# Two chunks a Schur or solve step, side steps placed by readiness, and a turn's gelus in four pieces

## The chip, the cores and the metric

The kernel runs on one core of one Trainium2 chip. The metric is the device time of one execution in microseconds. The kernel before takes 1141.81 us (median of three runs, 1141.43 to 1143.41).

## What is computed

The input `x` is 4 x 1024 x 256. It is normalized, and goes through an attention block with a norm of its own and 16 heads of 64; the block's input and the input itself are added. A second block is a feed-forward net with binarized weights and 1024 hidden units. Cut to what matters:

```python
# per batch and head, over 8 chunks of 128 rows (Qc, Kc, Vc: 128 x 64)
G = Kc.T @ Kc + 1e-4 * I
W = solve(G, Kc.T @ Vc)
U = I[:, :8]
for _ in range(2):
    U, _ = qr(W @ U)
S = 0.9 * S + U @ (U.T @ W)          # carried from chunk to chunk
out = 0.125 * (Qc @ S)
# block: x + layernorm(x) + out @ Wo, then
# x + (gelu(layernorm(x) @ bin(w1).T + b1) @ bin(w2).T + b2),  bin(w) = mean|w| * sign(w)
```

All of it is float32; the feed-forward products use float16 halves (a high and a low part) of the data.

## The kernel before, in words

There are 32 chunks of 128 rows (8 for each of 4 batches). The work has three kinds, and one list, `ORDER`, holds every step. Each engine's program walks through that same list and emits its part of each step, so the list fixes the order on every queue. `plan()` (line 55) makes the list on the host, with estimated durations (`PE_WEIGHT`, `ACT_WEIGHT`, `DVE_WEIGHT`) for TensorE, ScalarE and VectorE, and also picks a pair of the eight PSUM banks for each step: `put` (line 110) takes the pair that is free first.

**Stage 1**, per chunk c: `T` (transposes of the normalized rows), `K` and `V` (projections, line 1107, eight 512-column matmuls each), `G` (32 small gram matmuls, line 1127). ScalarE copies each result out of PSUM (lines 732, 740, 751), SyncE's queue stores the gram to DRAM (line 547).

**Side chains.** The 64 x 64 grams are inverted by halves. For a batch, VectorE eliminates the 32 x 32 leading blocks of all 128 lane-chunks at once (a *sweep*: `SLOAD`, 32 pivots `PIV` at lines 960 to 977, `SSTORE`; GpSimd's queue loads and stores it). Then each chunk goes through the *Schur chain* on TensorE: `LC` (load, lines 501 and 506), `SP`, `SX`, `SV` (lines 1155, 1168, 1180). The Schur complements are swept in a second sweep. Then each chunk goes through the *solve chain*: `LS` (load of lps, vv, rr and cu, lines 519 to 526), `S`, `U`, `W`, `Y`, `YT`, `Z` (lines 1190, 1200, 1214, 1225, 1234, 1244). Between two steps of a chain stands a copy by ScalarE. When the eight chunks of a batch are through, `MLOAD`, `SML`, `MSTORE`, `MI` invert an 8 x 8 matrix for every lane-chunk on VectorE (the *small inverse*, lines 989 to 1012) and bring the result back. There are eight sweeps, (0, b) for the leading blocks of batch b and (1, b) for its complements, in the order (0,0) (0,1) (1,0) (0,2) (1,1) (0,3) (1,2) (1,3). They use two buffers in turn.

**Turns**, one per chunk r: `LF`, `NZ` (line 1257), `WRA` and `WRB` (line 1271, the operator's two halves; VectorE adds each to the decayed state at line 1027, or copies it at line 1024), `Q` (line 1117), `OT` (line 1284, attention), `WO` (line 1295), the norm on VectorE (lines 1038 to 1053, with a power on GpSimd, line 684), `Y3` (line 1306), `HID` (line 1318), `GE0` and `GE1` (four gelus and a cast each, lines 855 and 860), `LO0` and `LO1` (GpSimd, line 669), `OUT` (line 1328) and its end on VectorE (lines 1058 and 1062). Four turns overlap: the loop over r places NZ and Q of r+2, OT of r+1, WO of r, HID of r-1 and OUT of r-2.

**Where side steps go.** `host` places a step of stage 1 or of a turn, and after every 1.7 us of planned TensorE time a *slot*: up to three Schur steps of three successive chunks, or, if no Schur work is open, up to two solve steps of two successive chunks. Loads have two buffers (four for gct), so that one chunk's data come while another's are used. Before the turns of a batch, `wait_for_batch` places slots and nothing else until the batch's small inverse is planned to be done.

## Time and profile before

| | |
|---|---|
| median of the runs | 1141.81 us |
| the profiled execution | 1141.08 us |
| its span | 1139.3 us, 41225 instructions |
| TensorE busy | 976.5 us (86%) |
| TensorE weight loads | 732.9 us (64%) |
| VectorE busy | 650.0 us (57%) |
| ScalarE busy | 536.2 us (47%) |
| GpSimd busy | 196.8 us (17%) |
| mean granted clock of TensorE | 0.916 of full speed |
| the chain that ended last | PE 73%, DMA 7%, ACT 7%, issue 5%, SP's queue 4%, VectorE 4% |

The span is the time between the first and the last instruction. PE is TensorE, PEld its weight loads, DVE VectorE, ACT ScalarE, POOL GpSimd, SPq the queue of SyncE, which issues most DMAs. The granted clock is a share of full speed: 1.0 is 2.4 GHz, 0.5 is 1.2 GHz, a value between them a mean over a stretch with both.

### The profile page before, as it was taken

What the parts mean: (1) busy time and instruction counts of PE and PEld (TensorE: products, weight loads), DVE (VectorE), ACT (ScalarE), POOL (GpSimd) and SP (SyncE); (2) the same over time, 40 slices, a digit from 0 to 9 for tenths busy, and PEclk for the clock granted to TensorE, in tenths of its full rate; (3) what the DMA queues carried; (4) which work ended last, traced back from release to release, by engine and by line L of the source; (5) the groups of instructions that cost most, each with busy time, mean ns of one, the idle gap of its engine ahead of it and who ended that gap; (6) DMA issues with size and microseconds to landing.
All of it is one profiled execution on the core that took longest, in us unless ns stands there. A gap on an engine that the chain in (4) does not pass through costs nothing.

```text
span 1139.3 us, 41225 instructions
## 1 busy us (share of the span) xinstructions
PE 976.5 (86%) x18210; PEld 732.9 (64%) x18210; DVE 650.0 (57%) x1439; ACT 536.2 (47%) x1064; POOL 196.8 (17%) x246
## 2 busy tenths in 40 slices
PE   4898898996889986567988899899578989999997
PEld 2454445653545555446877788687456878888886
DVE  5772980999669995153675676588321243333333
ACT  2653334633544554342545544356444544444445
POOL 3431000010020001000122132221000232222223
PEclk9999999998999996677998999899656999999999
DMA  9543126634664576443144321423444121111100
GB/s 289 165 142 93 56 88 155 168 120 109 169 170 96 155 187 183 101 109 88 51 139 126 98 66 41 118 64 93 133 101 103 56 53 40 40 41 40 40 20 20
DMA packets 210912, 117.49 MB, mean 103 GB/s; under 512 B 145776, under 2 KB 197360, under 8 KB 209712
## 3 DMA queue, kind: packets, MB, share of 16 engines
q1 hardware_dynamic: 205264, 93.62, 31.3%
q0 software_dynamic: 5472, 21.24, 6.1%
q8 instruction: 145, 2.38, 0.9%
q14 instruction: 31, 0.25, 0.1%
HBM read 61.74 MB, written 53.08 MB: 101 GB/s over the span
## 4 chain that ended last, share of the span: by engine, by line
PE 73%; DMA 7%; ACT 7%; issue 5%; SPq 4%; DVE 4%; POOL 1%; POOLq 0%; DVEq 0%; ACTq 0%
PE psum L1107 19%; PE psum L1295 10%; PE psum L1117 9%; PE psum L1127 5%; PE psum L1328 5%; PE psum L1318 5%; PE psum L1214 3%; PE psum L1284 3%; DMA cu<-gc_d 3%; DMA schur_mem<-lead_d 2%; PE psum L1271 2%; PE psum L1200 2%; PE psum L1180 2%; ACT kv L740 2%; PE psum L1155 2%
## 5 line engine op out<-in xcount | busy, mean ns | idle before, releaser
L1107 PE MATMUL psum<-wqkv,xhat 128*128 128x512 f32 x512 | 241.0, 621 | 2.5 <-ACT xhat L732 2.3
L968 DVE SCALAR_TENSOR_TENSOR outer<-sweep_mem,rd 128x992 f32<-128x992 f32 (+30 forms) x248 | 187.4, 755 | 8.7
L974 DVE TENSOR_TENSOR sweep_mem<-sweep_mem,outer 128x992 f32<-128x992 f32 (+30 forms) x248 | 177.7, 716 | 8.5
L1107 PEld LDWEIGHTS psum<-wqkv,xhat 128*128 128x128 f32 x512 | 97.2, 197 | 115.5 <-issue 112.8
L740 ACT COPY kv<-psum 128x1024 f32<-128x1024 f32 x64 | 64.8, 1012 | 164.7 <-PE psum L1107 164.7
L1295 PE MATMUL psum<-wo,kv 128*128 128x256 f32 x512 | 124.4, 398 | 0.7 <-DVE state L1027 0.4
L1117 PE MATMUL psum<-xhat,wqkv 128*128 128x128 f32 x1024 | 124.6, 281 | 0.3 <-ACT nz L829 0.3
L669 POOL TENSOR_TENSOR hsplit<-gc,hsplit 128x512 f16<-128x512 f32 x64 | 74.6, 1166 | 284.9 <-ACT hsplit L860 284.8
L1117 PEld LDWEIGHTS psum<-xhat,wqkv 128*128 128x128 f32 x1024 | 120.6, 197 | 2.0 <-ACT nz L829 0.4
L1295 PEld LDWEIGHTS psum<-wo,kv 128*128 128x128 f32 x512 | 98.5, 197 | 16.1 <-DVE state L1027 0.6
L855 ACT ACTIVATE gc<-psum,b1c,alpha 128x128 f32<-128x128 f32 x256 | 96.8, 468 | 19.1 <-PE psum L1318 19.1
L746 ACT COPY ql<-psum 128x1024 f32<-128x1024 f32 x32 | 32.4, 1012 | 105.6 <-PE psum L1117 105.5
L1127 PE MATMUL psum<-kv 128*64 128x128 f32 x1024 | 63.3, 275 | 18.3 <-ACT kv L740 17.8
L1027 DVE SCALAR_TENSOR_TENSOR state<-state,psum 128x256 f32<-128x256 f32 x56 | 22.7, 419 | 89.6 <-PE psum L1271 87.1
L1127 PEld LDWEIGHTS psum<-kv 128*64 128x64 f32 x1024 | 56.0, 137 | 24.8 <-issue 24.7
L1038 DVE TENSOR_TENSOR gc<-psum,resl 128x256 f32<-128x256 f32 x32 | 13.6, 425 | 98.0 <-PE psum L1295 98.0
L1328 PE MATMUL psum<-s2t,hsplit 128*128 128x256 f16 x512 | 65.3, 282 | 4.5 <-POOL hsplit L669 2.7
L1318 PE MATMUL psum<-y3t,s1t 128*128 128x128 f16 x1024 | 63.3, 220 | 0.8 <-ACT y3t L844 0.8
L838 ACT ACTIVATE kv<-psum 128x1024 f32<-128x1024 f32 x32 | 32.8, 1024 | 64.0 <-PE psum L1284 63.6
L1318 PEld LDWEIGHTS psum<-y3t,s1t 128*128 128x128 f16 x1024 | 58.0, 98 | 6.4 <-issue 6.2
L1328 PEld LDWEIGHTS psum<-s2t,hsplit 128*128 128x128 f16 x512 | 48.9, 101 | 15.4 <-issue 4.1
L1214 PE MATMUL psum<-cu,rr 64*64 64x64 f32 x1024 | 43.1, 262 | 14.7 <-ACT cu L798 14.7
(117 smaller groups left out, 1389.0 us busy)
## 6 DMA issues: line engine op xcount, KB each, us to landing
gc_d<-gc SPq DMA_DIRECT2D x32, 512.0 KB, 3.4
schur_mem<-gc_d SPq DMA_DIRECT2D x32, 384.0 KB, 3.9
f_d<-fac SPq DMA_DIRECT2D x32, 272.0 KB, 2.2
fl<-f_d SPq DMA_DIRECT2D x32, 272.0 KB, 2.9
sv_d<-sv SPq DMA_DIRECT2D x32, 192.0 KB, 2.8
lead_d<-sweep_mem POOLq DMA_DIRECT2D x4, 1024.0 KB, 5.1
schur_mem<-lead_d SPq DMA_DIRECT2D x64, 64.0 KB, 3.7
r_d<-pt SPq DMA_DIRECT2D x32, 128.0 KB, 2.0
```

Source lines behind the costliest of these rows:

```text
L669: nc.gpsimd.tensor_tensor(hsplit[:, r % 2, 1, t].rearrange("p t r -> p (t r)"), ht[:, BANK * n:BANK * (n + 1)], hsplit[:, r % 2, 0, t].rea ...
L740: nc.scalar.copy(kv[:, n], place(step, c)).then_inc(drain(step, c), 1)
L855: nc.scalar.activation(ht[:, P * t:P * (t + 1)], place("HID", r)[:, P * t:P * (t + 1)], ACT.Gelu, scale=alpha1[:, t:t + 1], bias=b1c[:, t: ...
L968: V.scalar_tensor_tensor(out=tile, in0=a[:, t, t + 1:HALF].unsqueeze(2).broadcast_to([P, m, HALF]), scalar=rd[:, t:t + 1], in1=a[:, t, t + ...
L974: V.tensor_tensor(rest, rest, tile, ALU.subtract).then_inc(swept, 1)
L1107: ins = mm(dst[:, cols], xnt[:, c, t], wqkv[:, n, t, cols], start=t == 0, stop=t == KT - 1)
L1117: ins = mm(dst[:, cols], wqkv[:, 2, t, cols], xnt[:, TURNS[r], t], start=t == 0, stop=t == KT - 1)
L1127: ins = mm(dst[side(a), P * h:P * (h + 1)], kv[:, 0, cols], kv[:, :, cols], start=True, stop=True)
L1214: ins = mm(dst[side(a ^ n), at:at + HD], u if turned else r, r if turned else u, start=True, stop=True)
L1295: ins = mm(dst[:, 0:DM], ot[:, r % 2, at:at + P], wo[:, h], start=h == 0, stop=h == PAIRS - 1)
L1318: ins = mm(dst[:, P * t:P * (t + 1)], s1t[:, k, P * t:P * (t + 1)], y3t[:, part, k], start=k + part == 0, stop=k + part == KT)
L1328: ins = mm(dst[:, 0:DM], hsplit[:, r % 2, part, t], s2t[:, t], start=t + part == 0, stop=t + part == FT)
```

## The change

- `K`, `V` and `Q` become two steps of one bank each (`KA`, `KB`, ...), each with its own copy of 512 columns. The gram's first half waits for the first halves only.
- Every Schur step and every solve step but `W` covers two chunks (a pair e). Its matmuls and copies are those of both, its stores one DMA. `W` stays per chunk. The load buffers hold one pair at a time (gct two pairs), so that a load waits for the steps of the pair before: lps and vv for U, rr and cu for the second W.
- `host` no longer counts TensorE time: after every hosted step one Schur step and one solve step may follow, each only if its input is planned to be there (`ready`).
- The plan waits for inputs (`ready` in `put`), its weights are new, and pivots may be planned up to 1.2 us ahead of TensorE (`DVE_BEHIND`).
- `GE0` and `GE1` become `GE0` to `GE3`, two gelus each, the cast of a half behind every second. They stand between the copies of other steps. `WRA` and `WRB` of r+2 move from the start of the next pass to behind `QB` and behind `Y3`.

The core of the diff:

```diff
-BANKS = dict(T=1, K=2, V=2, Q=2, G=2, FT=2, FB=1, SP=1, SX=1, SV=1, S=1, U=2, W=2, Y=2, YT=1, Z=2,
+BANKS = dict(T=1, KA=1, KB=1, VA=1, VB=1, QA=1, QB=1, G=2, FT=2, FB=1, SP=1, SX=1, SV=2, S=1, U=2, W=2, Y=2, YT=1, Z=2,
              NZ=1, WRA=2, WRB=2, OT=2, WO=1, Y3=1, HID=2, OUT=1)
-PE_WEIGHT = dict(T=.25, K=3.45, V=3.45, Q=3.6, G=1.8, FT=.9, FB=.4, SP=.6, SX=.7, SV=.9, S=.5, U=.5, W=1.1, Y=.4, YT=.4,
-                 Z=.4, NZ=.4, WRA=.4, WRB=.4, OT=1., WO=3.5, Y3=.3, HID=1.9, OUT=1.9)
-ACT_WEIGHT = dict(T=.9, K=1.2, V=1.2, Q=1.2, G=1.2, FT=1.2, FB=.5, SP=.5, SX=1.8, SV=.6, S=.3, U=1.3, W=1.2, Y=.5, YT=.3,
-                  Z=.6, NZ=.4, OT=1.2, Y3=.7, GE0=2.5, GE1=2.5)
-DVE_WEIGHT = dict(WRA=.5, WRB=.5, WO=1.5, X3=1.3, OUT=.95)
-SIDE_EVERY = 1.7
+PE_WEIGHT = dict(T=.4, KA=1.75, KB=1.75, VA=1.75, VB=1.75, QA=1.8, QB=1.8, G=1.9, FT=.9, FB=.5, SP=.9, SX=1.1, SV=1.5, S=.6, U=.85, W=1.05,
+                 Y=.55, YT=.5, Z=.65, NZ=.55, WRA=.45, WRB=.45, OT=1.05, WO=3.65, Y3=.35, HID=1.9, OUT=1.8)
+ACT_WEIGHT = dict(T=.95, KA=.6, KB=.6, VA=.6, VB=.6, QA=.6, QB=.6, G=1.05, FT=1.05, FB=.4, SP=.6, SX=2.4, SV=.85, S=.4, U=2.1, W=1.05,
+                  Y=.8, YT=.35, Z=.7, NZ=.4, OT=1.05, Y3=.6, GE0=.95, GE1=1.6, GE2=.95, GE3=1.6)
...
+POOL_WEIGHT = dict(LO0=1.25, LO1=1.25)
+DVE_BEHIND = 1.2
...
-            j, at = staged[0]
-            start = max(now["dve"], at)
-            if start > now["pe"]:
+            j, loaded = staged[0]
+            start = max(now["dve"], loaded)
+            if start > now["pe"] + DVE_BEHIND:
                 return
...
+    def follows(step, c):
+        return dict(KA=[("T", c)], KB=[("T", c)], VA=[("T", c)], VB=[("T", c)], G=[("VB", c)], SP=[("LC", c)], SX=[("SP", c)],
+                    SV=[("SX", c)], S=[("LS", c)], U=[("S", c)], W=[("U", c // 2)] if step == "W" else [],
+                    Y=[("W", 2 * c + 1)] if step == "Y" else [], YT=[("Y", c)], Z=[("YT", c)], NZ=[("LF", c)],
+                    WRA=[("NZ", c)], WRB=[("NZ", c)], OT=[("WRB", c), ("QB", c)], WO=[("OT", c)], Y3=[("X3", c)],
+                    HID=[("Y3", c)], OUT=[("LO1", c)]).get(step, [])
+    def ready(step, c):
+        return max([0.0] + [at.get(e, 1e9) for e in follows(step, c)])
...
-            now["pe"] = max([now["pe"]] + free[k:k + n]) + PE_WEIGHT[step]
+            k = bank(n)
+            now["pe"] = max([now["pe"], min(ready(step, c), now["pe"] + 20.0)] + free[k:k + n]) + PE_WEIGHT[step]
             before[step, c] = [u for i, u in enumerate(held[k:k + n]) if u and u not in held[k:k + i]]
...
+    def load_schur():
+        e = chain["schur_next"]
+        if e < NCH // 2 and at.get(("swept", 0, e // half_batch), 1e9) <= now["pe"]:
+            put("LC", e)
+            chain["schur"] += [("SP", e), ("SX", e), ("SV", e)]
+            chain["schur_next"] += 1
...
+    def schur_step():
+        if not chain["schur"]:
+            load_schur()
+        if not chain["schur"] or ready(*chain["schur"][0]) > now["pe"]:
             return False
+        step, e = chain["schur"].pop(0)
+        put(step, e)
+        if step == "SP":
+            load_schur()
+        elif step == "SV" and e % half_batch == half_batch - 1:
+            open_at[1, e // half_batch] = at["SV", e] + 4.0
         return True
+    def load_solve():
+        e = chain["solve_next"]
+        if e < NCH // 2 and at.get(("swept", 1, e // half_batch), 1e9) <= now["pe"]:
+            put("LS", e)
+            chain["solve"] += [("S", e), ("U", e), ("W", 2 * e), ("W", 2 * e + 1), ("Y", e), ("YT", e), ("Z", e)]
+            chain["solve_next"] += 1
+    def solve_step():
+        if not chain["solve"]:
+            load_solve()
+        if not chain["solve"] or ready(*chain["solve"][0]) > now["pe"]:
             return False
+        step, e = chain["solve"].pop(0)
+        put(step, e)
+        if step == "W":
+            if e % 2 == 0:
+                put(*chain["solve"].pop(0))
+            load_solve()
+        elif step == "Z" and e % half_batch == half_batch - 1:
+            put("MLOAD", e // half_batch)
+            small_at[e // half_batch] = now["pe"] + 7.0
         return True
     def side():
+        done = [schur_step(), solve_step()]
+        return any(done)
...
     def host(step, c):
         put(step, c)
-        main[0] += PE_WEIGHT.get(step, 0.0)
-        if main[0] >= SIDE_EVERY:
-            main[0] = 0.0
-            side()
+        side()
...
-        if on(r + 1):
-            put("WRA", r + 1)
-            put("WRB", r + 1)
         if on(r - 2):
             put("LO1", r - 2)
         if on(r):
...
         if on(r + 2):
             load_factors(r + 2)
             host("NZ", r + 2)
+        if on(r - 1):
+            put("GE1", r - 1)
         if on(r - 2):
             host("OUT", r - 2)
         if on(r - 1):
+            put("GE2", r - 1)
             put("LO0", r - 1)
         if on(r + 2):
-            host("Q", r + 2)
+            host("QA", r + 2)
+        if on(r - 1):
+            put("GE3", r - 1)
+        if on(r + 2):
+            host("QB", r + 2)
+            put("WRA", r + 2)
         if on(r):
             host("Y3", r)
-        if on(r - 1):
-            put("GE1", r - 1)
+        if on(r + 2):
+            put("WRB", r + 2)
     return order, sweep_order, where, before
...
+            def load_solve(e):
+                b, c = e // HALF_BATCH, 2 * e
+                if e == 0:
                     sp.wait_ge(eyes_placed, 4)
+                if e % HALF_BATCH == 0:
                     sp.wait_ge(sweep_stored[J[1, b]], 16)
+                    sp.wait_ge(sv_stored, 16 * HALF_BATCH * (b + 1))
+                    sp.wait_ge(r_stored, 16 * HALF_BATCH * (b + 1))
+                if e:
+                    sp.wait_ge(*is_filled("U", e - 1))
+                for i in range(2):
+                    sp.dma_start(lps[:, i], comp_d[b].rearrange("(s c q) t n -> c (q t) s n", c=CPB, q=QUADS)[c % CPB + i]
+                                 ).then_inc(solve_loaded, 16)
+                    sp.dma_start(vv[:, i], sv_d[c + i][:, :, HALF:]).then_inc(solve_loaded, 16)
+                if e:
+                    sp.wait_ge(*is_filled("W", c - 1))
+                for i in range(2):
+                    sp.dma_start(rr[:, i, :, 0:HALF], r_d[c + i]).then_inc(solve_loaded, 16)
+                src = gc_d[c:c + 2].rearrange("c (s u) r n -> r u c s n", u=2)
                 for a in range(2):
+                    for u in range(2):
+                        sp.dma_start(cu[rows(2 * a), u], src[rows(2 * a), u, :, :, HD:P]).then_inc(solve_loaded, 16)
...
+            def lower_rows(e):
+                act.wait_ge(*is_filled("U", e))
+                if e:
+                    act.wait_ge(*is_filled("W", 2 * e - 1))
                 for a in range(2):
                     sl = rows(2 * a + 1)
+                    ins = nc.scalar.copy(cu[sl].rearrange("p u c s n -> p (u c s n)"), place("U", e)[sl])
+                ins.then_inc(drain("U", e), 1)
 
...
+                half = n // 2
                 if n == 0:
                     act.wait_ge(*is_filled("HID", r))
-                wait(act, low_done, 2 * (r - 1) + n + 1)
-                for t in range(4 * n, 4 * n + 4):
+                wait(act, low_done, 2 * (r - 1) + half + 1)
+                for t in range(2 * n, 2 * n + 2):
                     nc.scalar.activation(ht[:, P * t:P * (t + 1)], place("HID", r)[:, P * t:P * (t + 1)], ACT.Gelu,
                                          scale=alpha1[:, t:t + 1], bias=b1c[:, t:t + 1]).then_inc(gelu_done, 1)
+                if n % 2 == 0:
+                    return
                 if r >= 2:
                     act.wait_ge(*is_filled("OUT", r - 2))
-                act.wait_ge(gelu_done, FT * r + 4 * n + 4)
-                nc.scalar.copy(hsplit[:, r % 2, 0, 4 * n:4 * n + 4].rearrange("p t r -> p (t r)"),
-                               ht[:, BANK * n:BANK * (n + 1)]).then_inc(drain("HID", r) if n else high_done, 1)
+                act.wait_ge(gelu_done, FT * r + 4 * half + 4)
+                nc.scalar.copy(hsplit[:, r % 2, 0, 4 * half:4 * half + 4].rearrange("p t r -> p (t r)"),
+                               ht[:, BANK * half:BANK * (half + 1)]).then_inc(drain("HID", r) if half else high_done, 1)
...
-                for h in range(PAIRS):
-                    for a in range(2):
-                        cols = side(2 * h + a)
-                        ins = mm(dst[side(a), P * h:P * (h + 1)], kv[:, 0, cols], kv[:, :, cols], start=True, stop=True)
+                for half in range(2):
+                    pe.wait_ge(*is_drained(("KA", "KB")[half], c))
+                    pe.wait_ge(*is_drained(("VA", "VB")[half], c))
+                    for h in range(4 * half, 4 * half + 4):
+                        for a in range(2):
+                            cols = side(2 * h + a)
+                            ins = mm(dst[side(a), P * h:P * (h + 1)], kv[:, 0, cols], kv[:, :, cols], start=True, stop=True)
                 ins.then_inc(fill("G", c), 1)
```

## Rows read from the trace of the kernel before

**Rows 1.** Windows: stretch, length, each engine's busy us, then granted clock, DMA share, GB/s.
```profile
417.00:520.00 103.00, 58.57 (x2394) 46.62 (x2397) 43.25 (x96) 42.32 (x94) 9.69 (x15) 0.66 0.58 146
...
795.00:868.00 73.00, 48.10 (x1749) 36.96 (x1746) 18.06 (x60) 31.78 (x70) 4.99 (x9) 0.57 0.49 118
933.00:1113.00 180.00, 172.94 (x2476) 153.20 (x2464) 60.60 (x136) 89.05 (x181) 44.21 (x50) 1.00 0.13 37
```

**Rows 2.** Timeline of TensorE in stage 1: start us, length us, what, idle before.
```profile
101.89 7.13 PE L1107 MATMUL psum<-wqkv,xhat 128*128 128x512 f32 x16
...
110.22 1.97 PE L1127 MATMUL psum<-kv 128*64 128x128 f32 x32 [0.98 <-ACT kv L740]
112.12 7.13 PE L1107 MATMUL psum<-wqkv,xhat 128*128 128x512 f32 x16
```

**Rows 3.** Waits: who waited for whom, us in total, times, longest us.
```profile
PE psum L1190 <- DMA cu<-gc_d: 33.3, 9, 6.4
...
PE psum L1155 <- DMA schur_mem<-lead_d: 22.1, 8, 7.6
...
PE psum L1127 <- ACT kv L740: 17.8, 19, 1.0
```

**Rows 4.** Timeline of TensorE: the first NZ, and two turns at the end.
```profile
519.91 1.04 PE L1257 MATMUL psum<-fl,mi 8*8 8x64 f32 x32 [5.53 <-issue]
...
1011.27 3.72 PE L1295 MATMUL psum<-wo,kv 128*128 128x256 f32 x16
...
1025.45 3.72 PE L1295 MATMUL psum<-wo,kv 128*128 128x256 f32 x16
```

**Rows 5.** Timeline of VectorE: first and last instruction of sweeps, and the first small inverse.
```profile
112.58 0.20 DVE L960 TENSOR_SCALAR sweep_mem<-sweep_mem 128x32 f32<-128x32 f32 x1 [18.46 <-DMA sweep_mem<-gc_d]
...
377.35 0.19 DVE L960 TENSOR_SCALAR sweep_mem<-sweep_mem 128x32 f32<-128x32 f32 x1
...
430.83 1.23 DVE L977 TENSOR_TENSOR sweep_mem<-sweep_mem,rd 128x1024 f32<-128x1024 f32 x1
...
479.82 0.16 DVE L989 RECIPROCAL mrd<-msw 128x1 f32<-128x1 f32 x1 [37.12 <-DMA msw<-f_d]
...
601.28 0.19 DVE L960 TENSOR_SCALAR sweep_mem<-sweep_mem 128x32 f32<-128x32 f32 x1
...
716.26 1.23 DVE L977 TENSOR_TENSOR sweep_mem<-sweep_mem,rd 128x1024 f32<-128x1024 f32 x1
```

**Rows 6.** Groups by form, ScalarE: busy us, mean ns of one, idle before.
```profile
L740 ACT COPY kv<-psum 128x1024 f32<-128x1024 f32 x64 | 64.8, 1012 | 164.7 <-PE psum L1107 164.7
...
L798 ACT COPY cu<-psum 32x512 f32<-32x512 f32 x64 | 36.9, 577 | 22.2 <-PE psum L1200 21.5
```

**Rows 7.** Timeline of TensorE in stage 1 with a Schur chunk, then with solve steps.
```profile
197.97 0.66 PE L1155 MATMUL psum<-schur_mem 32*32 32x32 f32 x30
...
199.96 0.44 PE L1096 MATMUL psum<-ident,xhat 128*128 128x128 f32 x2
...
360.40 1.97 PE L1127 MATMUL psum<-kv 128*64 128x128 f32 x32
...
373.05 1.97 PE L1127 MATMUL psum<-kv 128*64 128x128 f32 x32
```

**Rows 8.** The chain of waits, 470 to 480 us: a solve load with nothing beside it.
```profile
474.04 0.62 SPq L524
...
474.70 0.66 SPq L526
...
475.40 2.43 DMA cu<-gc_d
```

**Rows 9.** The chain of waits, 896 to 932 us: a small inverse, first and last.
```profile
910.72 0.41 ACT fac L823
...
926.84 0.06 DVE minv L1012
```

**Rows 10.** The chain of waits, 826 to 842 us: W products of two bare chunks.
```profile
830.79 2.02 PE psum L1214 x64
...
837.02 1.98 PE psum L1214 x64
```

More of the change, by code:

```diff
@@ L227, in load_factors @@
     def load_factors(r):
-        if 0 <= r < turns and r not in factors and ("Z", TURNS[r]) in where:
+        if 0 <= r < turns and r not in factors and ("Z", TURNS[r] // 2) in where:
             put("LF", r)
@@ new lines, in comp_inverse @@
+            def comp_inverse(e):
+                dst = begin("S", e)
+                pe.wait_ge(solve_loaded, 160 * (e + 1))
+                for c in range(2):
+                    for s in range(PAIRS // 2):
+                        at = HALF * (PAIRS // 2 * c + s)
+                        for q in range(QUADS):
+                            sl = rows(q)
+                            ins = mm(dst[sl, at:at + HALF], lps[sl, c, s, HALF:], lps[sl, c, s, 0:HALF], start=True, stop=True)
+                ins.then_inc(fill("S", e), 1)
@@ new lines, in lower_rows @@
+            def lower_rows(e):
+                dst = begin("U", e)
+                pe.wait_ge(*is_drained("S", e))
+                for c in range(2):
+                    for s in range(PAIRS // 2):
+                        for q in range(QUADS):
+                            at = BANK * (q % 2) + HD * (PAIRS // 2 * c + s)
+                            ins = mm(dst[rows(q | 1), at:at + HD], st[rows(q), c, s], vv[rows(q), c, s], start=True, stop=True)
+                ins.then_inc(fill("U", e), 1)
```

483 lines of the change are left out of this document (214 added, 269 removed).

## Prediction

> **What bounds the kernel now.** The profiled execution took 1141.1 us (span 1139.3; the median of the timed runs is 1141.8, so one may be set against the other). Section 1 of the page comes first: PE busy 86%, VectorE 57%, ScalarE 47%. The chain that ended last then says PE for 73% of its length, DMA 7%, ScalarE 7%. So TensorE's order of work is the kernel, and the question is where it is not busy or not at its full clock. The 40 slices point at two holes, and the windows give them numbers [rows 1]: 417 to 520 us, PE busy 58.6 of 103 us at a granted clock of 0.66, and 795 to 868 us, 48.1 of 73 us at 0.57; between 933 and 1113 us it is busy 172.9 of 180 us at 1.00. A clock of 0.57 is nearly all time at the lower of the two levels, 1.2 GHz. In both holes no turn runs: the order puts bare Schur and solve steps there, until the small inverse of batch 0, later of batch 2, is there. These two holes, not the matmuls, are what an order of work can win.
>
> Elsewhere the losses are small and regular. In stage 1 (projections and grams) one chunk takes 10.23 us, of which the gram waits 0.98 us for the copy of V [rows 2]; such waits are 17.8 us in all, and first loads of a batch or late loads make 22.1 and 33.3 us of PE waits [rows 3]. A turn without side steps takes 14.18 us [rows 4], and 7.1 idle us in 180 [rows 1] are 0.56 us of each, so its work is 13.6 us.
>
> VectorE's sweeps stand behind the holes. One sweep with nothing beside it takes 54.7 us; one between turns took 116 us [rows 5]. Eight sweeps follow one another, and the solve of a batch can't begin before its second sweep. In the same rows, VectorE stood still for 37.1 us at the first small inverse: its instructions stand in front of the pivots of the sweep begun at 432 us, which had no need to wait.
>
> **The change, part by part.**
>
> *K, V, Q in halves.* The matmuls are the same. The copies become two of 512 columns; from 1012 ns for 1024 columns and 577 ns for 512 [rows 6] a half takes about 0.58 us, so a pair costs ScalarE 0.15 us more: with ScalarE under half busy, nothing. The gram's first half no longer waits for the last copy: the transpose (about 0.3 us) and the first half gram (0.98) lie before that need, the copy ends about 0.8 us after V. The 17.8 us go. What is late next is PE itself: 9.25 us a chunk.
>
> *Two chunks a step.* PE runs the same matmuls: 2.0 us a chunk for a Schur chain (SP at 197.97 to its end at 199.96), about 3.2 for a solve chain (12.65 us from gram to gram with one solve chain inside, less 9.25, less a little for the copies) [rows 7]. ScalarE's U copy goes from four of 577 ns for two chunks to two of about 1.01 us [rows 6]; the other pairs save likewise, some 1.7 us a pair, hidden. The price is the buffers: lps, vv, rr, cu are now one set for the pair in work, not two sets in turn. The second half of a load (two rr, four cu) can be issued only when both W products of the pair before are filled. An rr issue takes 0.62 us of SP's queue and a cu issue 0.66, and the last cu lands 2.4 us later [rows 8]; six issues are up to 3.9 us, with the landing 6.3, and less where issues are shorter: 5 to 6.3 us from W to the next S. In between lie, on ScalarE and PE, the W copy, Y, YT and Z, which take about as long when bare. The order counts 5 us. I take 1 us lost a pair (bounds: 0, if a turn's step always lies between; 6.4, the longest such wait of before [rows 3]). Behind it on SP's queue stand only stores of later steps and LF and LR; these have a turn of slack.
>
> *Readiness instead of slots.* Before, a slot came after 1.7 us of main work and put up to three steps of a chain down whether their data were there or not, Schur always before solve. Now every main step is followed by at most one Schur and one solve step, and only if its input is due. Solve 0 no longer stands still while the Schur chain of batch 2 runs. That is the large effect, below. The first load of a batch is still tied to the planned end of its sweep. The planner counts the wait for V's copy before the gram, and PE will not wait there, so PE comes early; I count 4.5 us of wait for each of four such loads in stage 1, against 14 to 15 before.
>
> *WRA and WRB apart, gelus in four pieces.* WRB had to wait for the state update of WRA; Y3 and its own place now lie between. That is most of the 0.56 us a turn. Gelus: 4 x 0.47 us plus a cast as before, in the same order; Y3's and Q's copies may stand 1 us behind a piece, and their readers are later by more than that. Nothing.
>
> *Pivots up to 1.2 us ahead of PE.* They fill part of VectorE's idle time before each step of a turn. I take 105 us for a sweep between turns (bounds 90 and the old 116).
>
> **The sum.** Stage 1 ended at 417. Less 17.8 and 15 of waits, plus the Schur and solve chains that now fall in it (five chunks of 2.0, nearly four of 3.2: 22), plus 18 of first-load waits: 424. Sweeps: the first starts about 107 (112.6 less eight shorter chunks, held by the start-up), the second about 185, and from there one after another: 240, 295, 350, 404, and with the first small inverse 414. Solve 0 starts about 305 and gets its 24 to 30 places by 400, with 22 us for the small inverse (16 from the last factors' copy to its result [rows 9], 6 for its store and load). So the first turn starts at about 426, not 519.9 [rows 4]. Until then before had solved six more chunks (19 us): the clear gain is 75 us.
>
> Then sweep (0,3) to 519 and (1,2) to 624; solve 2 begins 10 us later. PE reaches the point where turn 16 is needed after 14.5 turns' work (198), solve 1 (25), Schur 3 (16), 12 of waits: 676. By then two pairs of solve 2 are done. Two are left, bare, at 2 x 6.2 us a pair [rows 10] plus 1: 27, plus the small inverse 22: 725. From there 17.5 turns' work (239), three pairs of solve 3 (19), 8 of waits, 4 at the tail and 5.5 from the last matmuls to the end: 1000.5, and 1.8 around the span: **1002 us**. Batch 3 costs no wait in this case: with PE bare its sweep ends near 704, its solve near 770, and turn 24 is needed after 830. Its own range, from the bounds of the sweep's pace and of the pair load: 975 to 1040.
>
> **Rivals.**
>
> *1. The other order of sweeps.* (1,2) and (0,3) become ripe within a few us of each other. With (1,2) first, solve 2 is early and there is no wait for batch 2, but Schur 3 lies between (0,3) and (1,3) with no sweep to run: (1,2) to 519, (0,3) to 624, Schur 3 and load to 684, (1,3) to 780. PE needs turn 24 at about 815; 2.7 pairs bare (36), the small inverse 22 and a late start make it 875, and ten turns (136) with the tail follow: 1020 us.
>
> *2. The holes stay.* Plan and chip drift apart: SP's queue sits at the first load of a batch, or VectorE at a small inverse, as in the 37 us of [rows 5]. Then only the regular parts are won: 17.8, 0.56 x 20 turns = 11, and half of 22.1 + 33.3: 1141 - 57 = 1085 us. For it speaks that the old planner too had thought its loads would be there; against it, that solve 0 no longer yields to Schur 2.
>
> *3. Slower: the single set of load buffers.* If a pair's load comes late at each of 16 solve and 16 Schur pairs, PE stalls there, mostly between turns. At 6.4 us, the longest of [rows 3], 32 of them are 205 us, less some 25 that fall into the wait for batch 2: 1180 us. It is slower than before from (1141 - 1002) / 32 = 4.3 us each. Against it: where a load was in time, a bare chunk took 6.2 us [rows 10], 12.4 a pair, and the load has the latter half of that. The granted clock speaks for a further price: with such waits among the matmuls it was 0.66 and 0.57 [rows 1]. The Trainium skill's page "TensorE: Matmul & The Clock Gate", section "HAM oscillation — how this bites in real kernels", says that DMA waits between bursts of matmuls make every burst start at half rate; by that rule each late load would also cost the step behind it up to double. The trace agrees in the two holes, and that is the rule that speaks against giving up the second set of buffers.
>
> **How the numbers follow.** Forecast 45%, rival 1 20%, rival 2 20%, rival 3 10%, anything else 5%. The range 960 to 1095 holds the first three. Anything within 0.2% (2.3 us) of before can't be told from no change; that is 2%, since no case lies there. Faster 88%, slower 10%.
>
> **What would show it.** PE timeline: first product of NZ near 426 us (step of readiness); 9.25 us from gram to gram before the first Schur step; turns of 13.7 us at the end. Windows: one hole instead of two, some 50 us long, before turn 16 (forecast) or turn 24 (rival 1). VectorE: 100 to 110 us a sweep between turns. Waits: S on cu loads, 10 to 20 us in all; 100 or more is rival 3. An NZ after 480 us would make the forecast wrong at its largest step.

## The result, and the profile after

The changed kernel takes 1065.17 us (median of four runs, 1064.58 to 1075.91) beside 1141.62 us for the kernel before on the same chip: a ratio of 0.935, 95% interval 0.929 to 0.941. The forecast was 1002 us in a range of 960 to 1095. So the sign and the range held, and the size was 63 us too good. The range had been drawn wide enough for two rivals: the forecast's own case, 975 to 1040 us, missed, and the number nearest to the result is rival 2's, 1085. In it both holes stay; they shrank to a third instead, though the causes that it names (SyncE's queue at the first load of a batch, VectorE at a small inverse) both showed. Run again on another chip the changed kernel took 1066.87 us (ratio 0.930, 0.927 to 0.933; one of these four executions, 1083.65 us at a lower clock, is left out of the ratio). The profiled execution took 1064.58 us.

The span and section 1 of the page, changed kernel:

```profile
span 1062.7 us, 41039 instructions
PE 945.8 (89%) x18210; PEld 717.6 (68%) x18210; DVE 663.3 (62%) x1439; ACT 529.0 (50%) x984; POOL 199.1 (19%) x246
```

Its windows, with the same columns as [rows 1]: stage 1 up to the last gram, the stretch to the first turn, the turns up to where batch 2 is waited for, that wait, the rest, and the lone turns near the end.

```profile
168.00:433.00 265.00, 234.31 (x4885) 145.38 (x4886) 202.12 (x373) 125.81 (x208) 15.03 (x21) 0.93 0.57 144
433.00:468.50 35.50, 13.03 (x580) 11.54 (x583) 15.99 (x45) 9.13 (x14) 6.72 (x10) 0.59 0.60 170
468.50:771.70 303.20, 275.60 (x7160) 240.90 (x7160) 225.65 (x458) 162.07 (x305) 67.02 (x81) 0.96 0.44 111
771.70:794.60 22.90, 13.70 (x521) 11.89 (x517) 6.80 (x26) 8.56 (x12) 2.60 (x3) 0.55 0.46 99
794.60:1062.70 268.10, 257.19 (x4277) 225.66 (x4276) 97.61 (x223) 142.09 (x296) 69.88 (x81) 0.99 0.17 48
860.00:1030.00 170.00, 167.77 (x2396) 148.27 (x2398) 70.23 (x159) 87.86 (x187) 45.53 (x52) 1.00 0.14 40
```

The two holes of [rows 1], 103 and 73 us long, are still two, but 35.5 and 22.9 us long, again at a clock of 0.59 and 0.55. Next, TensorE's timeline: a chunk of stage 1, from transpose to transpose, then the first product of NZ, and WO of two lone turns.

```profile
113.07 0.38 PE L1130 MATMUL psum<-ident,xhat 128*128 128x128 f32 x2
113.38 1.97 PE L1161 MATMUL psum<-kv 128*64 128x128 f32 x32
115.28 5.42 PE L1139 MATMUL psum<-wqkv,xhat 128*128 128x512 f32 x12
...
122.25 0.38 PE L1130 MATMUL psum<-ident,xhat 128*128 128x128 f32 x2
...
468.48 1.04 PE L1299 MATMUL psum<-fl,mi 8*8 8x64 f32 x32 [14.11 <-DMA fl<-f_d]
...
989.89 3.72 PE L1337 MATMUL psum<-wo,kv 128*128 128x256 f32 x16
...
1003.56 3.72 PE L1337 MATMUL psum<-wo,kv 128*128 128x256 f32 x16
```

A chunk takes 9.18 us, and the gram starts with no wait, where [rows 2] had 10.23 us and 0.98 of wait. The first NZ is at 468.48 instead of 519.91 [rows 4]; lone turns take 13.67 us instead of 14.18. The waits, with the columns of [rows 3]:

```profile
PE psum L1191 <- DMA schur_mem<-lead_d: 15.1, 5, 6.8
PE psum L1204 <- issue: 14.6, 8, 3.6
PE psum L1299 <- DMA fl<-f_d: 14.1, 1, 14.1
...
PE psum L1229 <- DMA cu<-gc_d: 2.0, 2, 1.7
```

The gram's 17.8 us are gone, and the waits of S (line 1229) on cu went from 33.3 to 2.0. Last, VectorE at the first small inverse:

```profile
411.73 0.29 DVE L1008 TENSOR_TENSOR sweep_mem<-sweep_mem,outer 128x128 f32<-128x128 f32 x1
451.06 0.17 DVE L1023 RECIPROCAL mrd<-msw 128x1 f32<-128x1 f32 x1 [39.03 <-DMA msw<-f_d]
```

Split at the first NZ and at the WO of turn 14 (turns are counted from 0), where the wait for batch 2 ends, the spans compare so. The third stretch ends with the span; the forecast's 725 is its end of the wait for batch 2.

| stretch | before | forecast | after |
|---|---|---|---|
| start to first NZ | 519.9 | 426 | 468.5 |
| to the end of the wait for batch 2 | 349.5 | 299 | 326.1 |
| to the end of the span | 269.9 | 275.5 | 268.1 |

So 51.4 us of the gain come ahead of the first turn and 23.4 in the middle. Against the forecast 42.5 us are missing ahead of the first turn and 27 in the middle, and 7.4 came back at the end.

### The profile page after: what moved, and what is told of

Its sections match the earlier page's. It is cut to its first block, busy times and chain, and to the rows that moved or that the text cites. A ratio compares the mean times of both kernels' runs of the same rounds, so it can differ in the third digit from the quotient of the medians.

```text
span 1062.7 us, 41039 instructions
## 1 busy us (share of the span) xinstructions
PE 945.8 (89%) x18210; PEld 717.6 (68%) x18210; DVE 663.3 (62%) x1439; ACT 529.0 (50%) x984; POOL 199.1 (19%) x246
## 4 chain that ended last, share of the span: by engine, by line
PE 66%; issue 12%; DVE 9%; DMA 7%; ACT 3%; SPq 3%; POOL 1%; POOLq 0%; DVEq 0%; ACTq 0%
PE psum L1139 11%; PE psum L1149 10%; PE psum L1337 10%; PE psum L1360 6%; PE psum L1370 5%; PE psum L1251 4%; DVE outer L1002 3%; PE psum L1326 3%; DVE sweep_mem L1008 3%; PE psum L1161 3%; PE psum L1312 2%; DMA schur_mem<-lead_d 2%; PE psum L1239 2%; PE psum L1299 2%; PE psum L1204 1%
## 5 line engine op out<-in xcount | busy, mean ns | idle before, releaser
L1139 PE MATMUL psum<-wqkv,xhat 128*128 128x512 f32 x512 | 246.7, 627 | 4.3 <-ACT xhat L758 4.3
L1008 DVE TENSOR_TENSOR sweep_mem<-sweep_mem,outer 128x992 f32<-128x992 f32 (+30 forms) x248 | 182.3, 735 | 8.5
L766 ACT COPY kv<-psum 128x512 f32<-128x512 f32 x128 | 75.1, 586 | 127.9 <-PE psum L1139 127.7
L1149 PE MATMUL psum<-xhat,wqkv 128*128 128x128 f32 x1024 | 128.2, 283 | 0.5 <-issue 0.3
L1337 PE MATMUL psum<-wo,kv 128*128 128x256 f32 x512 | 119.0, 385 | 0.0
L883 ACT ACTIVATE gc<-psum,b1c,alpha 128x128 f32<-128x128 f32 x256 | 103.6, 462 | 22.6 <-PE psum L1360 22.5
L1337 PEld LDWEIGHTS psum<-wo,kv 128*128 128x128 f32 x512 | 94.6, 190 | 13.7
L1161 PE MATMUL psum<-kv 128*64 128x128 f32 x1024 | 67.9, 287 | 3.4 <-issue 3.4
L1061 DVE SCALAR_TENSOR_TENSOR state<-state,psum 128x256 f32<-128x256 f32 x56 | 22.9, 418 | 65.7 <-PE psum L1312 65.7
L772 ACT COPY ql<-psum 128x512 f32<-128x512 f32 x64 | 37.3, 583 | 35.1 <-PE psum L1149 35.1
L1092 DVE TENSOR_TENSOR gc<-psum,alpha2r 128x256 f32<-128x256 f32 x32 | 13.5, 423 | 64.5 <-PE psum L1370 64.5
```

The lines of the kernel that those rows point to most:

```text
L766: nc.scalar.copy(kv[:, n, BANK * half:BANK * (half + 1)], place(step, c)).then_inc(drain(step, c), 1)
L883: nc.scalar.activation(ht[:, P * t:P * (t + 1)], place("HID", r)[:, P * t:P * (t + 1)], ACT.Gelu, scale=alpha1[:, t:t + 1], bias=b1c[:, t: ...
L1008: V.tensor_tensor(rest, rest, tile, ALU.subtract).then_inc(swept, 1)
L1139: ins = mm(dst[:], xnt[:, c, t], wqkv[:, n, t, BANK * half:BANK * (half + 1)], start=t == 0, stop=t == KT - 1)
L1149: ins = mm(dst[:, P * h:P * (h + 1)], wqkv[:, 2, t, cols], xnt[:, TURNS[r], t], start=t == 0, stop=t == KT - 1)
L1161: ins = mm(dst[side(a), P * h:P * (h + 1)], kv[:, 0, cols], kv[:, :, cols], start=True, stop=True)
```

## The experiments

All start from the changed kernel. The table puts the timed ones together. Besides the median and the ratio it has the time of the first NZ, the turn behind whose WO the last Z of batch 2 stands in the written order, the time from WO of turn 13 to WO of turn 14, and a lone turn. These last four are from the profiled executions. The runs came in groups, each on one chip with the kernel before beside it, which took 1139 to 1146 us; so ratios compare better than medians.

| kernel | median us | ratio to before, 95% | first NZ | last Z of batch 2 behind turn | turn 13 to 14 | lone turn |
|---|---|---|---|---|---|---|
| changed | 1065.2 | 0.935 (0.929-0.941) | 468.5 | 13 | 40.7 | 13.67 |
| the same again | 1066.9 | 0.930 (0.927-0.933) | 460.7 | 13 | 41.7 | 13.67 |
| one chain a host | 1054.2 | 0.925 (0.920-0.929) | 472.5 | 12 | 20.6 | 13.67 |
| gelus in halves | 1044.3 | 0.916 (0.911-0.921) | 458.7 | 12 | 22.7 | 13.67 |
| WR late | 1061.1 | 0.930 (0.925-0.936) | 462.5 | 13 | 41.6 | 13.31 |
| G waits for all | 1068.9 | 0.937 (0.932-0.942) | 469.5 | 13 | 40.9 | 13.67 |
| small inverse behind (1,1) | 1075.3 | 0.939 (0.937-0.942) | 461.4 | 13 | 41.4 | 13.67 |
| half a us of slack | 1077.0 | 0.941 (0.937-0.944) | 469.7 | 13 | 39.9 | 13.67 |
| two singles | 1075.8 | 0.938 (0.933-0.942) | 471.1 | 13 | 34.4 | 13.67 |
| all three back | 1041.4 | 0.912 (0.909-0.916) | 473.9 | 12 | 21.4 | 13.31 |
| small inverse inside (0,3) | 1068.5 | 0.936 (0.932-0.941) | 467.3 | 13 | 47.6 | 13.67 |
| pivots 2.5 us ahead | 1047.0 | 0.918 (0.914-0.922) | 464.8 | 11 | 19.2 | 13.31 |

**The same again.** A second look at the changed kernel, beside the three that follow it.

> The changed kernel, unchanged, beside the next three and before on one chip. Needed since two partial reversals were faster than it (1044 and 1054 against 1065 on another chip) and stage 1, which is the same program in all of them until the first turn, ended at 416 to 436. If those are effects of the edits: 1065 within 3. If the same kernel moves by 10 from chip to chip or load to load: anything from 1050 to 1080, and differences below 10 between kernels of separate calls say nothing.

It held within 2 us. But stage 1 ended between 423.5 and 433.0 in seven profiles that have one written order and one program there (the changed kernel's two among them), so differences in the first NZ below 10 us are not read as effects. The 416 of the expectation is the next kernel's, whose written order differs inside stage 1.

**One chain a host.**

```diff
-        done = [schur_step(), solve_step()]
-        return any(done)
+        return schur_step() or solve_step()
```

> A hosted step takes a Schur step if one is ready and a solve step only if none is, as before the change; pairs and everything else stay. Theory A (that both chains advance at one host brings the first turn forward): while batch 1 or 2 has its 12 Schur steps, batch 0's and 1's solve chain stands for about 24 us each, of which 12 or so come back later; first NZ at 480 instead of 468.5, total about 1077. Rival B (the pairs do it: a Schur turn of 12 steps is short and each step of a chain waits for its own eviction anyway, so the chains rarely want the same host): first NZ within 3 us of 468.5, total within 4 us of 1065.

The first NZ came at 472.5, 4 us behind the changed kernel's first profile, and the total was 11 us lower, not higher. Theory A fell; so did B on the total, as the next run explains. (The 11 us compare two chips; the ratio's interval, 0.920 to 0.929, still meets that of the repeat, 0.927 to 0.933.)

**Gelus in halves.** GE1 stands again right behind GE0, and GE2 and GE3 behind Y3.

> A turn's gelus go back to two places on ScalarE, after HID's host and after Y3's, as two blocks of 2.5 us in place of four of 0.95 and 1.6; pairs, half steps and WR's place stay. Theory A (the four pieces bring something only where small steps are hosted between turns, as their evictions wait behind a block of gelus): the lone turns at the end stay at 13.7 us, the stretches with solve steps between turns grow by about 0.3 us a turn on 16 turns, total 1065 to 1072. Rival B (OUT needs the first half's low part, which comes from the second piece: two pieces together free it earlier): turns 0.2 to 0.5 us shorter, total 1050 to 1058.

Lower still than B's 1050 to 1058, and not for B's reason: lone turns stayed at 13.67. What differs is the stretch before turn 14. TensorE's windows of the changed kernel's second run, of this one and of the one before, from 770 to 795 us:

```profile
770.00:795.00 25.00, 14.85 (x524) 12.44 (x525) 6.36 (x25) 8.81 (x13) 1.81 (x3) 0.66 0.40 88
```

```profile
770.00:795.00 25.00, 25.00 (x753) 21.93 (x752) 7.94 (x18) 14.91 (x26) 5.86 (x7) 0.98 0.39 95
```

```profile
770.00:795.00 25.00, 22.87 (x613) 19.88 (x608) 5.44 (x12) 13.12 (x25) 3.57 (x4) 1.00 0.41 102
```

14.9 us of work in 25 at a clock of 0.66, then 25.0 at 0.98 and 22.9 at 1.00: both edits removed the second hole. In the changed kernel it looks like this (TensorE's timeline, products of one kind cut to the first row):

```profile
772.85 0.34 PE L1251 MATMUL psum<-cu,rr 64*64 64x64 f32 x8 [1.12 <-ACT cu L823]
...
779.13 1.09 PE L1264 MATMUL psum<-ww 64*8 64x64 f32 x64 [1.19 <-ACT ww L830]
781.08 1.09 PE L1275 MATMUL psum<-ident,fac 128*128 128x128 f32 x4 [0.86 <-ACT fac L837]
782.62 1.18 PE L1286 MATMUL psum<-ww 64*8 64x72 f32 x64 [0.45 <-ACT ww L844]
784.15 1.08 PE L1229 MATMUL psum<-lps 32*32 32x32 f32 x64 [0.36 <-DMA cu<-gc_d]
785.80 1.93 PE L1239 MATMUL psum<-vv,st 32*32 32x64 f32 x64 [0.57 <-ACT st L814]
789.95 0.49 PE L1251 MATMUL psum<-cu,rr 64*64 64x64 f32 x8 [2.22 <-ACT cu L823]
```

Nothing in it waits for batch 2. These are W, Y, YT, Z, S, U and W of batch 3, one behind the other, each waiting for the copy of the step ahead of it (S, at 784.15, for its load); these waits are 6.8 us in all. NZ of turn 16, at 802.89, then started with no wait at all. The planner's loop `wait_for_batch` wrote them there: by its clock batch 2's inverse was not due, so it filled TensorE's order with side steps ahead of WO of turn 14. So what TensorE meets in the hole is a matter of the order.

That does not make the data of batch 2 early. GpSimd's and SyncE's timelines have the store of its small inverse and the load that spreads it:

```profile
781.07 0.59 POOL L680 DMA_DIRECT2D minv_d<-minv  x1 [8.53 <-DVE minv L1046]
...
784.97 2.46 SPq L597 DMA_DIRECT2D mi<-minv_d  x4
```

NZ of turn 16 stands 8.3 us behind WO of turn 14. Without the hole it would be due at about 780, before the inverse was stored. Batch 0 took 10.2 us from the inverse's result to its first NZ; by that, as an estimate, some 11 of the 22.9 us would have come back as a wait for data, had only the side steps been moved.

**WR late.** WRA and WRB return to the start of the next pass, ahead of WO.

> WRA and WRB go back to the start of the next pass, just ahead of WO; all else stays. Theory A (forecast's term: WRA and WRB ahead of Y3's place take 0.5 us off each turn, as their evictions on VectorE then lie beside Y3 and WO): last turns 14.1 to 14.2 us instead of 13.67, and total 1065 + 32 x 0.45 = about 1079. Rival B (the shorter turn comes from the halves of Q and the banks they leave, WR's place being indifferent): turns within 0.1 us of 13.67, total within 4 us of 1065.

Theory A had the wrong sign. A lone turn got shorter, 13.31 us. The timeline of one says why:

```profile
988.63 0.39 PE L1348 MATMUL psum<-ident,x3split 128*128 128x128 f16 x4
988.94 0.59 PE L1312 MATMUL psum<-nz,fl 8*64 8x64 f32 x32
989.46 0.92 PE L1337 MATMUL psum<-wo,kv 128*128 128x256 f32 x3
```

The two WR steps together are one burst of 0.59 us, with no wait; apart, in the changed kernel, they are 0.46 each, and between them stands Y3. So [rows 4]'s 14.18 became 13.67 in spite of their new place, not by it. That they no longer wait must go back to something else in the change (the halves of Q or the choice of banks, say; no run tells).

**G waits for all.** The gram waits for the four copies ahead of its first product.

> G waits for all four copies of K and V before its first matmul, in place of two before each half; the half steps stay. Theory A (the halves bring it by being evicted while the next half is multiplied, and by the hosted step and T that lie between VB and G): the last copy is 0.6 us long and ends before G starts, so G's waits stay near zero and the total within 4 us of 1065. Rival B (the wait per half is what hides the last copy): 0.5 us a chunk on 31 chunks, stage 1 ends at 448 instead of 433, total about 1078.

The gram waited 0.55 us where nothing hides it (12.5 us in 22 waits), a chunk of early stage 1 took 9.80 us, and stage 1 ended at 436. The total moved by 2 to 4 us: what stage 1 loses is mostly taken up by later waits. So of the 1.05 us a chunk that the change won there, the wait for each half is worth 0.62 us (9.80 less 9.18); the other 0.43 is left for the copying in halves, which no run took away alone.

**The small inverse behind (1,1).** VectorE's instructions of an inverse are held back until the sweep under way has ended.

> VectorE's part of a small inverse is placed behind the last pivot of the sweep under way instead of in its middle; nothing else moves. Theory A (the 39 us that VectorE stood in sweep (1,1) delay sweeps (0,3) and (1,2) and so turn 16's data, and TensorE's bare wait at 772 comes from it): (1,1) ends near 423, (1,2) near 612 instead of 649, the wait of 23 us goes, total about 1040 to 1045. Rival B (solve 2 goes at 25 us a pair beside turns and sets turn 16, sweep (1,2) being slack): (1,2) earlier, but the last turn of batch 1 is followed by a wait of 15 us or more all the same, total 1058 or more.

Sweep (1,1) ended at 414.0, but its stand moved only behind it, 29.1 us long, since the sweep had 5 us left. (1,2) ended at 649.9, and turn 16's hole stayed. The total was 8 us above the changed kernel's on the same chip, with the ratios' intervals apart (0.937 to 0.942 against 0.927 to 0.933); what brought them is not known. As the stand was only moved, the question comes again below.

**Half a us of slack.**

```diff
-        if not chain["solve"] or ready(*chain["solve"][0]) > now["pe"]:
+        if not chain["solve"] or ready(*chain["solve"][0]) > now["pe"] + 0.5:
```

and the same for the Schur chain.

> The planner places a chain's next step when its operands are due within 0.5 us of TensorE's time, not only when they are there; in the plan's own times every second host between turns went without a step for 0.1 to 0.9 us. Theory A (the 25 us a solve pair are 12 hosts, half of them empty): solve pairs of batch 0 and 2 take 15 to 19 us, the first NZ comes at 445 to 455 instead of 468, turn 16's wait is halved or gone, total 1035 to 1050; each step may cost 0.1 to 0.3 us of waiting on ScalarE. Rival B (the pairs' pace is set by their loads through single buffers): the pace stays at 25 us a pair, S waits 2 to 4 us on its data, total 1060 to 1075.

Neither. The pairs of solve 2 went a little faster, some 21 us from S to S on average (682 to 746) against 24.6 (664 to 738), and S waited 3 us for data in these four, which speaks against B there. But stage 1 ended at 449.9 instead of 426.6: three more side steps lay in it (60 instead of 57), and TensorE waited 11 us longer in it, up to 5.0 at one load of S. Sweep (1,2) ended at 666.8, and the last Z of batch 2 stood behind turn 13 as before.

**Two singles.** Each pair step is two single-chunk steps, one behind the other, with a bank, an access pattern and a copy of its own; loads and buffers are the pairs'. The expectation says that the order stays too, but it did not: the planner's weights were halved with the steps, and in the order that came of it solve 2 begins behind turn 9 instead of 8. ScalarE runs 176 instructions more. From the planner:

```diff
         put(step, e)
+        put(*chain["schur"].pop(0))
```

> Order, loads, stores and buffers of the pairs stay, but every pair step is two single-chunk steps one behind the other, each with its own bank, its own eviction and the single chunk's accesses, as before the change (some 250 more ScalarE instructions). Theory A (pairing pays by fewer and longer evictions and no wait between two halves): ScalarE busy 30 to 40 us more, 0.3 to 0.5 us a step of a chain more latency, total 1070 to 1085. Rival B (what pays is the order, a step of each chain a host; the two singles even overlap eviction and multiplication): within 5 us of the changed kernel of this call.

ScalarE was busy 22 us more (551.0), and the total was 9 us above the changed kernel's on the same chip (ratios 0.938 and 0.930, the intervals just apart). That is within theory A's range, but it isn't the pairs' alone: stage 1 ended at 447.7 instead of 426.6, as in the run with slack, and S waited 16.2 us on its loads instead of 2.0 in the first profile of the changed kernel. What the pairs bring as such is not shown.

**All three back.**

> The three edits that, taken back alone, made the changed kernel no slower are taken back together: one chain a host, gelus in halves, WRA and WRB at the start of the next pass. What is left of the change is the pairs, the halves of K, V and Q, G's two waits and the planner's model. Theory A (their prices add: 12, 22 and 5 us by the runs so far): total 1025 to 1032. Rival B (they all paid by the same thing, the bare wait of 23 us before turn 16, which can go only once): 1040 to 1048, with a first turn at about 470 and no bare wait.

Rival B: 1041.4. The three prices don't add: one chain a host and gelus in halves each remove the same hole.

**More loads in the last turns.** From turn 21 on, each OUT is followed on SyncE's queue by four loads into a dead buffer.

> The changed kernel; from turn 21 on each turn also loads four chunks' Gram rows (4,096 pieces of 384 bytes, 1.57 MB) into a buffer that nobody reads any more; some 115 GB/s in a stretch that has 43. TensorE stood 33.7 to 42 us in 30 or so gaps of 1 to 2 us that no semaphore ends, nearly all where small steps stand beside turns and the core moves 110 to 170 GB/s; in the last turns there are none. Theory A (TensorE's instructions come late because their fetches share the DMA engines with the small pieces): such gaps appear in the last turns, 1 to 2 us a turn or more, which lengthens them from 13.67 to 15 or more. Rival B (the gaps come from the density of matmuls of 30 ns beside turns alone): turns stay at 13.67 within 0.1, no such gap.

Its windows 880 to 940 and 940 to 1030 us, then the latter of the changed kernel:

```profile
880.00:940.00 60.00, 60.00 (x887) 52.77 (x888) 23.00 (x51) 29.79 (x62) 15.51 (x18) 1.00 0.14 40
940.00:1030.00 90.00, 90.00 (x1284) 79.57 (x1271) 33.57 (x71) 48.42 (x104) 23.70 (x26) 1.00 0.62 148
```

```profile
940.00:1030.00 90.00, 90.00 (x1300) 79.82 (x1302) 34.16 (x73) 48.55 (x103) 23.80 (x27) 1.00 0.13 38
```

At 148 GB/s instead of 38, TensorE was busy without a gap and turns stayed at 13.67 us (the total of 1074.1 has the last loads at its end). Theory A's forecast for these turns failed: traffic of this kind makes no gap there. Whether it does beside dense small products was not tried; the last section says why that matters.

**The small inverse inside (0,3).** GpSimd loads sweep (0,3) ahead of the inverse's matrices, and VectorE's part stands behind two pivots of (0,3).

> The run with the small inverse behind sweep (1,1) only moved VectorE's stand by 5 us, since the sweep had 5 us left: its question is asked again. Here the load of small inverse 0 stands behind the load of sweep (0,3) on GpSimd's queue, and VectorE's part behind the first two pivots of (0,3), so (1,1) and (0,3) are not held up by it. Theory A (forecast's reason for the missing 61 us): (0,3) starts at about 445 instead of 462 and ends at 505 to 515 instead of 538, (1,2) ends at about 625 instead of 649, turn 16's bare wait goes from 23 to under 8 us, total 1045 to 1052. Rival B (turn 16's data are set by the pace of solve 2 beside the turns): (1,2) earlier by 15 or more, yet total within 6 us of 1066.

VectorE's timeline: the end of (1,1), and the start of (0,3).

```profile
412.39 1.23 DVE L1031 TENSOR_TENSOR sweep_mem<-sweep_mem,rd 128x1024 f32<-128x1024 f32 x1
442.48 0.20 DVE L1014 TENSOR_SCALAR sweep_mem<-sweep_mem 128x32 f32<-128x32 f32 x1 [28.87 <-DMA sweep_mem<-gc_d]
```

(1,1) ended at 413.6 instead of 461.9, and (0,3) started at 442.5 instead of 461.8. Yet (0,3) ended at 535.8 (538.2 in the changed kernel), (1,2) at 650.2 (649.2), and the total was 1068.5. Neither theory had this: the 19 us were lost again inside the two sweeps. Their pivots stand in VectorE's order between steps of given turns, so they go at the turns' pace, whenever they start. VectorE still stood 28.9 us, now for the load of (0,3), so the run takes away the stand inside (1,1) and not all standing.

**Pivots 2.5 us ahead.** Gelus in halves, WR late, and DVE_BEHIND at 2.5 instead of 1.2.

> Gelus in halves and WRA and WRB at the start of the next pass, both chains at a host as in the changed kernel, and DVE_BEHIND 2.5 instead of 1.2: the planner lets VectorE's pivots run 2.5 us ahead of TensorE's time, which puts the first step of solve 2 behind turn 6 instead of 8 and its last behind turn 11 instead of 13. Theory A (what sets turn 16's wait is behind which turn of the written order solve 2 stands; the bare wait goes when it ends two turns early): no bare wait, first turn near 460, total 1025 to 1036, the best of all. Rival B (pivots ahead of a turn's evictions hold up the turns, and turns that solve 2 no longer meets are not there for solve 3): TensorE's waits on VectorE rise from 7 to 20 us or more, or a wait stands before turn 24, total 1042 to 1060.

(1,2) ended at 630.0, 19 us earlier than in the changed kernel. But with gelus in halves alone it had ended at 634.7, so only 5 us can be put down to the pivots, though the last of them now stands behind turn 5 instead of 7 in the written order. There was no hole before turn 14. But 1047.0 us is no better than gelus in halves alone (ratios 0.918 and 0.916): from turn 3 to turn 4 it took 47.7 us (30.9 in the changed kernel), with 6.9 us of wait for a Schur load in it and 7.6 of gaps without a releaser. TensorE's waits on VectorE behind stage 1's start were 9.9 us, against 6.2 with gelus in halves. Theory A's mechanism held (no hole when solve 2 ends early), its total did not; the total is in B's range.

## Why the prediction was off, step by step

*K, V in halves: right.* 9.25 us a chunk was forecast, 9.18 came, and the 17.8 us went.

*Pairs: right in what they don't cost.* Waits of S on cu were to be 10 to 20 us and were 2.0. Rival 3, 4.3 us a pair, is excluded. What pairs bring by themselves was counted at nothing, and no run shows it.

*The first turn at 426: wrong by 42.5 us, the larger part of the error,* though below the 480 us that the prediction named as its limit. The forecast had solve 0 done by 400, 22 us for the small inverse, and stage 1's end at 424 beside it. Stage 1 ended at 433 in this profile (same order: 423.5 to 433.0). The last Z of solve 0 ended at 434.9. A pair took some 25 us, about as forecast; it was the first S that stood at 333 instead of 305. Its sweep ended at 304.7 instead of 295 and was stored by 309.3, its first load left SyncE's queue only at 321.9, right behind the store of a Schur pair, and the last of its ten pieces was issued by 329.8. And the way from the last Z to the first NZ was 33.6 us, not 22. So about 28 of the 42.5 us come from the late first S and 12 from the way. The parts of the way, from SyncE's, GpSimd's and VectorE's timelines:

```profile
434.49 2.73 SPq L527 DMA_DIRECT2D schur_mem<-gc_d  x2
437.26 1.67 SPq L532 DMA_DIRECT2D schur_mem<-lead_d  x2
438.98 2.19 SPq L588 DMA_DIRECT2D f_d<-fac  x1
...
460.31 1.49 SPq L597 DMA_DIRECT2D mi<-minv_d  x4
```

```profile
445.70 2.33 POOL L676 DMA_DIRECT2D msw<-f_d  x4 [83.29 <-DMA f_d<-fac]
...
458.55 0.57 POOL L680 DMA_DIRECT2D minv_d<-minv  x1 [7.07 <-DVE minv L1046]
```

4.1 us until the store of the last factors is issued (a pair's load stood ahead of it on SyncE's queue), 6.7 until it has landed and the load of the inverse is issued, 5.4 for that load, 7.2 for the inverse, 10.2 to store it, spread it and start NZ. The prediction had taken 16 us from the last copy to the inverse's result, by [rows 9], and 6 from there to NZ. Here the first part took 23.3, of which 4.1 are the queue, and the second 10.2. The same way was 29.0 to 38.8 us in the other runs.

*"VectorE at the small inverse" (rival 2's mechanism): there, and harmless.* VectorE stood 39.0 us, as in the 37.1 of [rows 5], and I had taken its absence into the sum. The run that puts the inverse inside (0,3) takes the stand away from sweep (1,1), which ends 48 us earlier, and the time stays. This is the reason that I would have named from the profile alone, and it is wrong.

*105 us for a sweep between turns: of the right size.* The two took 76 and 111 us, in the order that the forecast had (rival 1 did not come), and solve 2 began at 664 instead of 634.

*The wait for batch 2: the step with the wrong mechanism.* The forecast had 49 us bare: two pairs of solve 2, then the small inverse. Measured are 22.9 us with neither in them: side steps of batch 3 that the planner put ahead of turn 14, because in its own time batch 2 was late. From the end of solve 2's last Z, 764.9 us, to where the load that spreads the inverse was issued, 787.4, it took 22.5 us, much as forecast, but that time lay beside a turn and beside the hole. In every kernel whose last Z of batch 2 stands behind turn 13 the hole is there, turn 13 to 14 takes 34 to 48 us and the ratio to before is 0.930 to 0.941; where it stands behind turn 12 or 11, turn 13 to 14 takes 19 to 23 us and the ratio is 0.912 to 0.925. These kernels differ in more than the place of the side steps: where the last Z stands earlier, the inverse is there earlier as well (its load was issued at 760.5 to 769.1 us in the four without a hole, at 780.5 to 795.4 in the others). No run moved the side steps alone, so how much of the hole is the order's and how much the late data's is open; the estimate above gives the data about half. The four gelu pieces and the second chain a host had tipped the plan over this edge. By the planner's code, pieces between the copies make it hold each copy to be later and leave the next host empty; this step was read, not measured.

*The middle otherwise: three terms too small.* From the first NZ to the hole it took 303 us, forecast 250. The four pairs of solve 2 lie in it, at 6.2 us each (S 0.75, U 1.10, two W 2.09, Y 0.82, YT 0.60, Z 0.84): 25 us. The sum had none there and two in the hole, though it says itself that two are done by then: 12 us left out. (Its parts also add up to 677 where it says 676, and rival 3's to 1182 where it says 1180.) Gaps of TensorE were 27 us instead of 12, 20 of them without a releaser. And at a granted clock of 0.96, 276 us of work are, by estimate, 11 longer than at 1.00. In the holes the clock was 0.59 and 0.55. The Trainium skill's rule that was weighed there ("TensorE: Matmul & The Clock Gate", "HAM oscillation — how this bites in real kernels") speaks of waits for loads between bursts of matmuls. The first hole agrees, with 14.1 of its 22.5 idle us in one wait for a load; in the second only one wait of 0.36 us was for a load, 6.4 us were for ScalarE's copies and 2.4 without a releaser.

*The edits counted at nothing.* "Most of the 0.56 us a turn" was ascribed to WR's new place, which costs 0.36 a turn; the gelu pieces, "nothing", cost the most of all, by way of the plan. Read as a whole the change's gain is that of the run with all three back: halves of K, V and Q, pairs, and steps placed when ready. The rest of it takes some 24 us away again (1065.2 against 1041.4; by the ratios, 0.930 and 0.935 against 0.912, 20 to 26).

## What to carry to other kernels

Where a planner writes the order, an edit that changes no engine's work can still move the time by 2%, by tipping a step over a turn's border; compare the written orders first, and look for side steps that stand bare ahead of a main step which waits for nothing. Then look when that step's data came, before the order is given the whole price. An engine that stands still for 39 us is a cause only if what is behind it comes earlier when the stand is taken away. A way through two stores and two loads is summed part by part, the queue ahead of each included. And a reversal whose planner is left free to write another order tests that order too.

## What the runs showed of the hardware that was not expected

TensorE stood still without a releaser in 32 gaps of up to 3.6 us, 42.3 us in all (24.1 in 20 before the change), nearly all in stretches with many small products (64 of S take 0.75 us, 32 of a gram 1.97): 7,160 matmuls in 303 us here, 2,396 in 170 us in the lone turns, which have none. One of them, inside a single W whose 128 products are all in the record:

```profile
774.99 0.49 PE L1251 MATMUL psum<-cu,rr 64*64 64x64 f32 x5
777.25 0.37 PE L1251 MATMUL psum<-cu,rr 64*64 64x64 f32 x2 [1.76 <-issue]
```

The trace says more than the timed runs do. Number TensorE's recorded instructions, weight loads included, in order of start: the instructions at all 32 gaps have a number that leaves 193 or 194 when divided by 256. In the fourteen profiles of this case 397 of 403 such gaps leave 193 to 195. A gap is likelier, the faster the 256 instructions ahead of such a place went. In the changed kernel there was one at 15 of 17 places where they took 2.5 us or less, at 17 of 79 where they took 2.5 to 6.75, and at none of 48 where they took longer. In the lone turns they take 6.8 us or more. So the matmuls themselves are not what stands still; the reading is that TensorE gets its instructions in blocks of 256, and that a gap is a block which comes late. That the blocks are late for DMA traffic is neither shown nor excluded: the run with more loads had nearly four times the traffic, but only beside lone turns, where each block has time enough.

And one burst of 32 small products of WR takes 0.59 us, two bursts of 16 with another step between them 0.92.
